# Two routed expert layers in 32 whole and 7 half tiles, with the second layer's tiles started before its last row scatters are done

## The reference, cut to what matters

```python
x = x + ffn0(scan(cond, x, W, b, alpha))      # scan: 256 steps of h = tanh(h*(1-alpha) + sigmoid(h@Wh.T + z@Wz.T + b)*z)
x = x + ffn1(mixture(x, cond, ...))

# ffn0: 8 experts, every token goes to its 2 best
h1    = relu(einsum('th,ehf->etf', xt, w1) + b1)          # 256 -> 1024
out_e = einsum('etf,efh->eth', h1, w2) + b2               # 1024 -> 256
out   = einsum('eth,te->th', out_e, mask)                 # mask: 1 for the 2 chosen experts
# mixture: a shared expert for all tokens, and 8 small experts, 2 per token, with gates
shared = (silu(x @ sw1.T) * (x @ sw3.T)) @ sw2.T          # 256 -> 512 -> 256
H      = gelu(x @ rw1[e].T)                               # 256 -> 128 -> 256
out    = (shared + sum over the 2 experts of gate * (H @ rw2[e].T)) / 3
# ffn1: a dense layer, activations rounded to 8 bits with one scale from the maximum of the whole input
```

## Time and profile before

| | us |
|---|---|
| median of 3 runs | 1201.23 (1199.84 to 1202.0) |
| the profiled execution | 1204.75 |
| its span, first to last instruction | 1202.9 |
| scan, to the first product of the expert tiles | 377.6 |
| first expert layer, 377.6 to the last product | 412.7 |
| from there to the mixture's first tile (915.5) | 125.2 |
| mixture tiles, 915.5 to 1027.2 | 111.7 |
| from there to the overall maximum (1087.4) | 60.2 |
| dense layer, to the end | 115.5 |

### The profile page before, as it was taken

The page is one execution under the profiler, slowest core; times in us unless marked ns, Lnnn a source line. Parts: engine busy times, 40 slices in busy tenths (PEclk is TensorE's granted clock), DMA queues, the critical chain, the costliest instruction groups (busy, mean ns, idle before and its releaser), DMA issues.

```text
span 1202.9 us, 30907 instructions
## 1 busy us (share of the span) xinstructions
PE 1023.2 (85%) x10073; PEld 805.0 (67%) x10085; DVE 823.5 (68%) x2840; ACT 548.2 (46%) x1736; POOL 389.3 (32%) x428
## 2 busy tenths in 40 slices
PE   6777777777777999999999999967678999667898
PEld 5656656566565888888888888854355787433355
DVE  5676777776776778985555555528664777777887
ACT  4555555555554333333333333343425767114376
POOL 1002112111123666243333333315773667202000
PEclk9999999999999999999999999979898999978999
DMA  8313323233233578555444443374246998530024
GB/s 231 102 58 103 90 89 103 83 99 102 76 107 107 88 140 165 101 84 67 66 66 57 62 64 60 59 200 161 89 140 207 281 291 280 198 121 0 1 36 105
DMA packets 127354, 136.49 MB, mean 113 GB/s; under 512 B 62337, under 2 KB 102146, under 8 KB 127042
## 3 DMA queue, kind: packets, MB, share of 16 engines
q1 hardware_dynamic: 104770, 93.34, 29.4%
q0 software_dynamic: 22464, 41.61, 15.3%
HBM read 74.43 MB, written 58.70 MB: 111 GB/s over the span
## 4 chain that ended last, share of the span: by engine, by line
PE 66%; DVE 14%; ACT 9%; issue 5%; POOL 3%; DMA 3%; SPq 0%; DVEq 0%; POOLq 0%; ACTq 0%
PE ps L1395 17%; PE ps L1405 17%; PE ps L646 10%; PE ps L2011 8%; DVE ps L1940 6%; PE ps L2016 5%; ACT work L1864 4%; ACT ps L1859 4%; POOL mrows L1331 2%; DVE imax L1253 2%; PE ps L1981 2%; PE ps L731 2%; PE ps L1162 1%; PE ps L1167 1%; PE ps L1133 1%
## 5 line engine op out<-in xcount | busy, mean ns | idle before, releaser
L1423 ACT ACTIVATE lane<-ps,b_now 128x256 f32<-128x256 f32 x312 | 147.6, 473 | 260.3 <-PE ps L1395 248.4
L1395 PE MATMUL ps<-lane,W 128*128 128x256 f16 x1872 | 213.1, 274 | 0.9 <-issue 0.9
L1405 PE MATMUL ps<-W,lane 128*128 x1872 | 210.7, 273 | 0.2 <-DVE lane L1498 0.2
L1395 PEld LDWEIGHTS ps<-lane,W 128*128 x1872 | 183.9, 98 | 24.0 <-issue 1.7
L1405 PEld LDWEIGHTS ps<-W,lane 128*128 128x128 f16 x1872 | 182.8, 98 | 22.1 <-issue 0.8
L1572 POOL DMA_INDIRECT results<-lane,dest x78 | 125.2, 1605 | 216.7 <-DVE lane L1486 180.5
L2011 PE MATMUL ps<-work 128*128 128x16 f16 x2048 | 98.8, 177 | 86.1 <-ACT work L1864 85.4
L2011 PEld LDWEIGHTS ps<-work 128*128 128x128 f16 x2048 | 76.1, 106 | 137.8 <-ACT work L1864 136.3
L1498 DVE TENSOR_TENSOR lane<-lane 128x256 f16<-128x256 f32 x312 | 133.1, 427 | 10.8
L1542 POOL DMA_INDIRECT rows<-work,slot_of x64 | 63.1, 987 | 156.4 <-DVE ps L1940 152.4
L1496 DVE CAST lane<-lane 128x256 f16<-128x256 f32 x312 | 93.5, 300 | 20.5 <-ACT lane L1423 20.5
(11 more groups left out here) (260 smaller groups left out, 1660.2 us busy)
## 6 DMA issues: line engine op xcount, KB each, us to landing
W<-mrows SPq DMA_DIRECT2D x39, 260.0 KB, 3.9
stage<-rweights SPq DMA_DIRECT2D x39, 256.0 KB, 3.7
stage<-in_w1T SPq DMA_DIRECT2D x16, 512.0 KB, 3.8
stage<-in_w2T SPq DMA_DIRECT2D x16, 512.0 KB, 4.1
b_now<-in_b SPq DMA_DIRECT2D x39, 128.0 KB, 2.9
work<-in_zT SPq DMA_DIRECT2D x32, 128.0 KB, 2.3
results<-in_xn SPq DMA_DIRECT2D x32, 128.0 KB
W<-results SPq DMA_DIRECT2D x8, 512.0 KB, 4.5
```

Of the source, the lines that this page charges most:

```text
L1395: last = pe.matmul(ps[:, f % 4, 0:ST], of_e(W1[:, bass.ds(e, 1), a, k, f * P:(f + 1) * P]), xT[:, p, b, k], start=(i == 0 and k == 0), sto ...
L1405: last = pe.matmul(ps[:, 4 + q, 0:D], hid[:, a, f, q * P:(q + 1) * P], of_e(W2[:, bass.ds(e, 1), b, f]), start=(i == 0 and f == 0), stop=( ...
L1423: act.activation(v4[:, f % 4], ps[:, f % 4, 0:ST], ACT.Relu, bias=b1_now[:, p, f:f + 1], scale=A_SCALE / W_SCALE).then_inc(l1_v, 1)
```

## The change

It has five parts. (1) Both expert layers keep 32 whole tiles and add 7 tiles of one block of 128 slots, the last of all; a table of two segments per expert says where whole pairs and odd blocks lie (28 operations for it rather than 17). (2) The mixture builds its table in an early and a late part, like the first layer; the first 16 tiles need the rows of steps 0 to 2 alone, and tile 16 is the first that waits for step 3's. The late part runs three operations per tile inside the tiles. All 8 groups have their own row buffer, so no step waits for `moved`. (3) Units are dealt out anew: 6, 9, 12 and 14 in the steps (41 before the tiles, not 44), 45 in the tiles (two in each of the first seven), 10 behind them. (4) Inside a step the transposes of the next groups stand at another place, and in step 0 all 32 router operations run ahead of the units. (5) x and `mresults` are read by two DMAs per group rather than one; groups are combined in order and the last group's shared output is written by ScalarE.

```diff
-SLOT_TILES = (PAIRS + E * (ST - 1)) // ST
+HT = ST // 2
+UNITS_MAX = (PAIRS + E * (HT - 1)) // HT
+WHOLE_TILES = PAIRS // ST
+HALF_TILES = UNITS_MAX - 2 * WHOLE_TILES
+SLOT_TILES = WHOLE_TILES + HALF_TILES
-STEP_UNITS = 8
-BRIDGE_UNITS = 12
-TILE_UNITS = 30
-LATE = 6
-COMBINE = (0, 1, 2, 6, 3, 4, 5, 7)
+STEP_AT = (0, 6, 15, 27, 41)
+TAIL_UNIT = UNITS * GROUPS - 10
+PADS_AT = 2
 def tile_units(n):
+    upto = lambda n: min(STEP_AT[STEPS_M] + min(2 * n, n + 7), TAIL_UNIT)
+    return range(upto(n), upto(n + 1))
...
+        def blocks_of(n):
+            return 1 if is_half(n) else SQ
...
# mixture_pe, one step
-                for k in range(3):
-                    shared(v + k)
+                for v in steps_units(m, 0, 3):
+                    shared(v)
                 mix_ranks(m)
-                for k in range(3, 6):
-                    shared(v + k)
-                for g in (2 * m + 2, 2 * m + 3):
-                    if g < GROUPS:
-                        transposes(g)
-                    shared(v + 4 + g - 2 * m)
+                if m < STEPS_M - 1:
+                    transposes(2 * m + 2)
+                for v in steps_units(m, 3, 5):
+                    shared(v)
+                if m < STEPS_M - 1:
+                    transposes(2 * m + 3)
+                for v in steps_units(m, 5):
+                    shared(v)
...
# experts_pe
-                            last = pe.matmul(ps[:, f % 4, 0:ST],
-                                             of_e(W1[:, bass.ds(e, 1), a, k, f * P:(f + 1) * P]), xT[:, p, b, k],
+                            last = pe.matmul(ps[:, f % 4, 0:wide],
+                                             of_e(W1[:, bass.ds(e, 1), a, k, f * P:(f + 1) * P]), xrows[:, b, k],
-                        for q in range(SQ):
+                        for q in range(blocks_of(n)):
...
# sync: mixture rows, weights, and the reads of the results
-            for i in range(XBUFS):
-                sp.wait_ge(moved[i], 2 * GT * 16 * ((GROUPS - 1 - i) // XBUFS + 1))
+            for m in range(STEPS_M - 1):
+                sp.wait_ge(moved[m], 4 * GT * 16)
             load_rows_of(0)
+                if n == EARLY:
+                    sp.wait_ge(mtable_ready, 2)
+                    sp.wait_ge(padded, 16 * E)
+                    sp.wait_ge(moved[STEPS_M - 1], 4 * GT * 16)
+            for g in range(GROUPS):
+                src = mresults_d[2 * GN * g:2 * GN * (g + 1)].rearrange("(q p k) d -> p q k d", p=P, k=2)
+                for k in range(2):
+                    sp.dma_start(routed[b][:, :, k], src[:, :, k]).then_inc(routed_in[k][b], 16)
```

More of the change, by code:

```diff
@@ L118 @@
 C_CEIL = C_FLOOR + E
-C_LANE = C_CEIL + E
+C_REGION = C_CEIL + E
+C_LANE = C_REGION + E
 C_TOKEN = C_LANE + 1
@@ L198, in build_program @@
         wq_n = wq_flat.rearrange("p (m n) -> p m n", m=2)
+        xrow = [a.rearrange("p (b q n) -> p b q n", b=GROUPS // 2, q=GT)
+                for a in (xsn_flat, work[:, 3072:3072 + GROUPS // 2 * GT * MROW])]
         part = carve(work[:])
@@ L363, in build_program @@
         mw_used = sem("mw_used")
-        x_in = [sem(f"x_in{i}") for i in range(2)]
+        x_in = [sem(f"x_in{i}") for i in range(4)]
         mix_start = sem("mix_start")
@@ L392, in build_program @@
         m16_zero = sem("m16_zero")
-        moved = [sem(f"moved{i}") for i in range(XBUFS)]
+        moved = [sem(f"moved{i}") for i in range(STEPS_M)]
         spare_rows = sem("spare_rows")
@@ L556, in early_table_op, with late_table_op @@
             else:
-                dve.tensor_copy(room_of[:, 0:K].rearrange("p (n a) -> p n a", a=1), now[:, 1]).then_inc(table_ready, 1)
-        def late_table_op(dve, n):
-            K = SLOT_TILES - EARLY
+                dve.tensor_scalar(rooms[:, 0:K].rearrange("p (n a) -> p n a", a=1), now[:, 1], 2.0, None, ALU.mult)\
+                   .then_inc(ready, 1)
+        def late_table_op(dve, n, t):
+            step, ready, experts, rooms = t
             now = tile_f[:, :, EARLY:]
+            whole, half = place[:, 0:LATE_WHOLE], place[:, LATE_WHOLE:]
+            region = cst[:, C_REGION:C_REGION + E]
+            p2, o = segs[:, 0:E], segs[:, E:]
@@ L607, in is_tile, with is_half, stored_by @@
+            ins.then_inc(step, 1)
         def is_tile(n, k):
             return isinstance(n, int) and n == k
+        def is_half(n):
+            return isinstance(n, int) and n >= WHOLE_TILES
+        def blocks_of(n):
+            return 1 if is_half(n) else SQ
+        def stored_by(n):
+            return 16 * sum(blocks_of(k) for k in range(n % 2, n + 1, 2))
         def psh(b):
@@ L807, in mixture_act @@
                 act.activation(dst, psb(3 + n), ACT.Copy).then_inc(wt_cp, 1)
+            act.wait_ge(rw_out, 16)
+            for a in range(2):
+                tokens(a)
             for g in range(2):
```

604 lines of the change are left out of this document (330 added, 274 removed).

## The result

The changed kernel takes **1169.61 us** (median of 4, 1169.22 to 1170.88) against 1200.87 for the kernel before on the same chip (4 runs, 1199.84 to 1202.0): ratio 0.9741, 95% interval 0.9725 to 0.9758. The forecast was 1152, with 1138 to 1168 around it. It is faster, but 17.6 us slower than forecast. The profiled execution took 1169.48, a span of 1167.7; the one of before had 1204.75, which is 3.9 above the median of these runs, so between the two profiled executions 35.3 us are saved and between the medians 31.3.

The account below looks back on a forecast made before the run. TensorE was taken to bound the expert and mixture tiles, chains of waits the mixture's steps. Experts' -35.8 and mixture's -13.3 sum to -49.1 us, from the median 1201.23 to 1152.1; range 1138 to 1168.

Parts of the forecast that it names:

- seven half tiles: First expert layer: a half tile takes 5.4 us instead of a whole tile's 10.48, saving 35.6 us over seven.
- table operations in tile 2: First expert layer: 16 of the table's 28 operations fall in tile 2, making VectorE late, +0.9 us.
- two of its own signs: The forecast falls if experts save under 25 us; last seven expert tiles should start 5.3 to 5.6 us apart.
- over 6 is B: Sign in the last seven expert tiles: starts over 6 us apart would mean Rival B.
- Rival B: Expert half tiles cost more than half, 6.4 to 7.4 us, through handoffs or weight loads: 1164, chance 0.13.
- The boundary: End of the expert layer: one scatter less and a smaller result save 2.1 us; the routed weights' write costs 1.
- The steps: Mixture's steps: 102.2 us, 3 of it for lower clock; tiles start at 909.6, 5.9 us earlier.
- some 6 us ahead of the low half: Mixture's steps 1 and 2: TensorE idles some 6 us ahead of the first transposes' low half; without it, Rival A.
- Rival A: Mixture's steps run at the rate of the queues, not the chain, 87 rather than 102 us: 1137, chance 0.15.
- The tiles and the tail: Mixture's tiles take 125.2 us, ending at 1034.8; the combination behind them ends at 1074.1 instead of 1087.4.
- Rival C: The mixture gives nothing: steps and tiles take what the tail loses, through waits, low clock and slow reads: 1166, chance 0.14.
- Rival D: Mixture's tiles run at TensorE's lower clock level behind long waits: slower, 1270 if throughout, chance 0.03.

Follow-up runs that it names:

- experiment 1: Changed kernel, but the seven half tiles of the first expert layer multiply with expert 0's weights at a constant place: 1159.65 us, ratio 0.9647.
- experiment 2: Changed kernel, but all tiles of the first expert layer multiply with expert 0's weights at constant places: 1159.88 us, ratio 0.9656.
- experiment 3: Changed kernel with each half tile of the first expert layer placed behind a whole one instead of all seven at the end: 1166.05 us, ratio 0.9698.
- experiment 5: Changed kernel with the split of x for the next step moved ahead of the units ending the step before: 1158.37 us, ratio 0.9631.
- experiment 6: On top of experiment 5, TensorE's ranks behind the next group's transposes and more units (two units in step 0): 1155.43 us, ratio 0.9627.
- experiment 8: Changed kernel with units where they stood before (8 per step, 12 ahead of the tiles, 30 in them, 22 behind), combination not interleaved: 1185.83 us, ratio 0.9877.
- experiment 7: Changed kernel, but the mixture's first tile waits for the row scatters of all four steps instead of three: 1188.60 us, ratio 0.9896.
- experiment 4: Changed kernel with the 2 MB write of the routed weights issued at tile 14 of the first expert layer: 1170.75 us, ratio 0.9735.
- experiment 9: On top of experiment 5, the 2 MB write of the routed weights moved behind the tenth read of x: 1158.63 us, ratio 0.9633.
- experiment 10: Changed kernel with experiments 3, 5, 6 and 9 together in one kernel: 1147.98 us, ratio 0.9551.

## Why the prediction was right or wrong

The terms, in us, from the two profiled executions:

| term | forecast | measured |
|---|---|---|
| seven half tiles | -35.6 | -24.3 (49.1 instead of 73.4) |
| table operations in tile 2 | +0.9 | +1.3 |
| start of the layer, not touched (0.5 later, its first pass 1.0 shorter) | 0 | -0.4 |
| last scatter and write: last product to reads of x | -1.1 | +0.3 (7.0 instead of 6.7) |
| reads of x to the mixture's first tile | -5.9 | -3.4 (115.1 instead of 118.5) |
| mixture's tiles | +13.5 | +12.0 (123.7 instead of 111.7) |
| behind them, to the end of the combination | -20.9 | -20.4 (39.8 instead of 60.2) |
| sum | -49.1 | -34.9 |

Another 0.3 us fall behind the combination. By two of its own signs the forecast fails: the experts' stage saves 23.1 us, less than the 25 it asked for, and the half tiles start 7.1 to 7.3 us apart (the first 6.1), where "over 6 is B".

**The half tile is the step that failed**: "a half tile is 48 x 56 = 2.7 plus 24 x 109 = 2.6, together 5.3 us", taken as 5.4, measured 7.0, 11.3 of the 14.2 us missed between the profiles. The prediction took 56 ns from the transposes and named the doubt that "theirs is one identity operand". The products of experiment 1 show both numbers, 56 and 109, exactly, for weights that differ each time. What the transposes don't have is a place of the weights that is only known at run time. With it a product takes 90 ns in a row of half tiles, without it 56 (experiment 1), and in whole tiles nothing shows under 109 (experiment 2). In the program the six products of a column use four different places, which TensorE's own instruction list has to work out; they stood there before the change as well, and the prediction gave them no term. That these computations are what takes the time fits all three experiments, but stays argued. Rival B had the right size (6.4 to 7.4 us a tile, 1164) for wrong reasons: neither the handoffs nor the weight loads by themselves do it, since both are the same in experiment 1.

The first half tile was at 3.2 us where the others were at 4.3, and experiment 3 gave all seven 3.2 to 3.4 by putting a whole tile in front of each.

**Another 3.6 us are the reference.** The sum, made in the profiled execution of before, was taken off the median, which lies 3.5 lower; that supposes that the changed kernel's profiled execution lies as far above its own median. It lies 0.1 below. That is chance, not a step of the change.

**The boundary** was mis-sized: -2.1 for a scatter less and +1 for the write, in sum -1.1, came to +0.3. The scatter beside the write landed after 8.8 us, and the last one waited for it. The forecast also took the scatters' own chain at 4.1 us a tile and so under 5.3; experiment 1 shows it at 4.6 to 5.4, with a delay from the last whole tile ahead of it. At 5.3 us a tile that chain is nearly as long as the tiles, and what holds up one scatter is hardly made up.

**The steps** were right in kind and 2.2 us short in length (104.4 against 102.2). The first units of the four stand 18.0, 27.8 and 32.1 us apart (784.53, 802.56, 830.33, 862.39), where 17.7, 26 and 30 were forecast before the low clock was added. The wait of "some 6 us ahead of the low half" was 5.4 and 4.7; experiment 5 removes just that and gains 13.2 us of the steps, the two waits and the low clock behind them. Rival A, that the steps run at the rate of the queues, is excluded for this order; with the split early they still take 91 and not 87, with TensorE waiting for the ranks or, once these are moved, for VectorE to read the banks (experiment 6).

**The tiles and the tail** came within 1.5 us each, and the combination at 3.66 us a group (3.64 forecast). But the prediction argued the tiles' 125.2 as a sum of independent parts (0.95 for a half tile, 1.31 for a unit). Experiment 8 shows that the sum holds only where a unit stands in each tile; without one ScalarE's copy, the rows and the clock set a half tile at 2.3 to 2.9. The changed kernel has a unit beside nearly every tile, and there the sum fits: tiles stand 4.35 us apart with two units and 3.05 with one (4.5 and 3.2 forecast, the start of the stage spread over them), half tiles 2.2. That the 0.95 came true is in so far luck. From the last tile to the combination it is 10.3 us now and 26.9 in experiment 8, for 4.0 us more in the tiles. These 16.6 can't be set against the 20.4 gained behind the tiles, because the kernel before combined between its units and experiment 8 doesn't. The overlap with the last scatters is worth 19 (experiment 7). Undone one by one, the two cost 35, while the mixture as a whole gained 11.8: the new order needs both, and neither figure is a gain over the kernel before.

Rival C (1166) was nearest in time, but by its mechanism it did not happen: from the reads of x on the mixture gave 11.8 of 13.3. Rival D did not happen either: the granted clock in the tiles is 1.00.

## What to carry to other kernels

When a tile is made smaller, ask for each engine what of its list does not shrink: here the run-time places of the weights, free at 256 columns and, by experiments 1 and 2, the bound at 128. Take the price of an operation from a row with the same kind of operand and address, not only of the same shape, and where short pieces must have run-time addresses, put long ones between them. Work that fills waits is worth a trial move before its price is argued: the same unit cost 0.27 us in the tiles and its full 1.31 behind them, and ranks moved behind more units only moved the wait to the next bank.

## What the runs showed of the hardware

- A product of 128 columns with fresh weights takes 56 ns at full clock with constant places and about 90 with run-time places in a row of half tiles (experiment 1). In whole tiles a product of 256 columns takes 109 either way (experiment 2); the 24 of a half tile's second layer take some 0.2 us longer together with run-time places.
- Behind a whole tile (96 products of 256 columns) the next 48 of 128 columns at run-time places take 3.2 to 3.4 us instead of 4.3, and the whole tile behind them stays at 10.5 (experiment 3).
- In the last tiles a scatter that adds 128 rows of results lands in 3.6 to 5.2 us, in 6.0 where it came second behind its neighbour (experiment 1, 721.19), and in 7.7 to 8.8 when a write of 2 MB from another queue is issued beside it. Moved away from the write (experiments 4, 9 and 10), none that something waited for took over 5.2.
- TensorE's granted clock behind waits: 0.50 behind 4.7 us of waiting, where 12 products of 512 columns took 5.16 us (843.7 to 848.5), and 0.59 behind 12.9 us, where they took 4.54 (experiment 7). At 1.00 they take 2.75.
